# A fused LayerNorm, attention and mixture-of-experts kernel: other groups, and another engine, for the LayerNorm scale and shift of the prologue

## The reference

```python
x = hidden_states                                  # (8, 512, 128)
xn = (x - mean(x)) / sqrt(var(x) + 1e-5)           # over the last axis
s  = attention(xn)                                 # 8 heads of 16; then its own norm, Wo, bo
# the two experts of a token come from its first two normalised elements:
h   = mod(int(xn[:, 0] + xn[:, 1]), 8)
sel = (h, mod(h + 1, 8))
g  = silu(sum over e in sel of 0.5 * (relu(xn @ W1[e] + b1[e]) @ W2[e] + b2[e]))
out = x + s * g
```

## Time and profile before

| what | value |
|---|---|
| time, median of 3 runs | 422.58 us (422.43 to 423.55) |
| time of the profiled execution | 423.16 us |
| its span, first to last instruction | 421.3 us |
| TensorE busy in the span | 389.6 us (92%) |
| VectorE | 300.1 us (71%) |
| ScalarE | 268.5 us (64%) |
| GpSimd | 153.2 us (36%) |

### The profile page before, as it was taken

How to read it: one execution, slowest core, us unless ns; L and a number is a source line. 1 busy time by engine, 2 the same in 40 slices (tenths; PEclk the granted TensorE clock), 3 DMA queues, 4 the chain that set the end, 5 groups by cost and what they waited for, 6 DMA issues and landing times.

```text
span 421.3 us, 8389 instructions
## 1 busy us (share of the span) xinstructions
PE 389.6 (92%) x2575; PEld 249.2 (59%) x2576; DVE 300.1 (71%) x793; ACT 268.5 (64%) x667; POOL 153.2 (36%) x188
## 2 busy tenths in 40 slices
PE   4986979999999999999999999999999999999984
PEld 1343868655676657666665668666666657663322
DVE  6797886667687766866676768766686767766884
ACT  3571556666667765577765767576665668575783
POOL 7753302172235442374335421642353232420100
PEclk9997799999999999999999999999999999999997
DMA  7974763244305640235504540344255141214840
GB/s 243 343 226 116 196 217 90 75 112 140 133 13 167 197 143 14 77 109 160 186 16 130 173 137 18 128 137 157 61 163 172 25 161 49 78 19 127 299 165 25
DMA packets 36946, 54.76 MB, mean 130 GB/s; under 512 B 6724, under 2 KB 25141, under 8 KB 36903
## 3 DMA queue, kind: packets, MB, share of 16 engines
q1 hardware_dynamic: 31456, 46.94, 33.5%
q0 software_dynamic: 3296, 6.76, 7.6%
q10 hardware_dynamic: 2151, 0.53, 0.6%
HBM read 15.59 MB, written 6.75 MB: 53 GB/s over the span
## 4 chain that ended last, share of the span: by engine, by line
PE 76%; DVE 11%; ACT 4%; issue 4%; DMA 2%; POOL 2%; DVEq 0%; ACTq 0%; POOLq 0%
PE ring L1383 14%; PE ring L1404 14%; PE pv_bank L1317 13%; PE score L1279 13%; PE exp L1304 11%; DVE neg_max L1034 4%; PE ring L1241 2%; PE ring L1343 2%; PE ring L1266 2%; PE ring L1325 1%; ACT hT L813 1%; ACT xin L775 1%; DMA qs<-max_rows 1%; DMA xs<-xn_rows,inverse 1%; PE ring L1365 1%
## 5 line engine op out<-in xcount | busy, mean ns | idle before, releaser
L1034 DVE TENSOR_REDUCE neg_max<-score 128x1 f32<-128x512 f32 x256 | 170.7, 685 | 70.2 <-PE score L1279 65.3
L1279 PE MATMUL score<-ks,qs 96*128 96x512 bf16 x256 | 98.4, 388 | 8.6 <-DVE neg_max L1034 7.4
L775 ACT ACTIVATE xin<-exp 128x512 f32<-128x512 f32 x120 | 70.1, 604 | 39.0 <-PE exp L1304 36.2
L1304 PE MATMUL exp<-qs,ks 99*128 99x512 bf16 x244 | 91.8, 380 | 3.2 <-ACT xin L775 1.5
L813 ACT ACTIVATE hT<-ring,pair 128x128 f32<-128x128 f32 x256 | 73.5, 375 | 28.1 <-PE ring L1383 25.4
L775 ACT ACTIVATE probs<-exp 128x512 f32<-128x512 f32 x124 | 72.8, 611 | 28.3 <-PE exp L1304 26.9
L679 POOL DMA_INDIRECT y_rows<-y_sb,inverse x32 | 32.0, 999 | 137.8 <-DVE y_sb L1166 136.6
L1404 PEld LDWEIGHTS ring<-w_sb,hT 128*128 128x128 f32 x568 | 74.2, 193 | 8.7 <-issue 2.1
L1404 PE MATMUL ring<-w_sb,hT 128*128 (+1 forms) x568 | 76.4, 278 | 0.8 <-ACT hT L813 0.8
L1383 PEld LDWEIGHTS ring<-xsT,pair 128*128 128x128 f32 x512 | 65.1, 191 | 13.8 <-issue 7.9
L1383 PE MATMUL ring<-xsT,pair 128*128 128x128 f32 x512 | 69.4, 278 | 0.5 <-issue 0.5
(11 more groups left out here) (195 smaller groups left out, 409.3 us busy)
## 6 DMA issues: line engine op xcount, KB each, us to landing
pair<-table SPq DMA_DIRECT2D x32, 580.0 KB
qs<-parts SPq DMA_DIRECT2D x42, 128.0 KB
ks<-parts SPq DMA_DIRECT2D x42, 128.0 KB
xin<-_attn_hidden_states_dram SPq DMA_DIRECT2D x8, 256.0 KB, 5.5
table<-in_L_ffn_W_dram SPq DMA_DIRECT2D x2, 1024.0 KB, 9.8
w_sb<-in_L_ffn_W_dram SPq DMA_DIRECT2D x8, 256.0 KB, 6.1
xn_rows<-xn SPq DMA_DIRECT2D x8, 256.0 KB, 3.1
table<-_attn_hidden_states_dram SPq DMA_DIRECT2D x8, 256.0 KB, 4.7
```

Source lines behind the costliest of these rows:

```text
L775: a.activation(prob(n), exp_banks[n][:, :], ACT.Exp, scale=SCALE).then_inc(exp_done, 1)
L1034: v.tensor_reduce(neg_max[:, b % 2, col:col + 1], score_bank[n % 2][:, :], AX.X, ALU.max, negate=True).then_inc(max_taken, 1)
L1279: t.matmul(score_bank[n % 2][:, :], qs[0:MAX_ROW, b % STK, hh, c * P:(c + 1) * P], ks[0:MAX_ROW, b % STK, hh, :], start=True, stop=True).t ...
L1304: t.matmul(exp_banks[n][:, :], ks[0:KROWS, b % STK, hh, kc * P:(kc + 1) * P], qs[0:KROWS, b % STK, hh, :], start=True, stop=True).then_inc ...
```

## The change

The groups become five (batch 0, batch 1, batches 2 and 3, 4 and 5, 6 and 7), with a step time for each. For all groups but the last, `shift` is computed on GpSimd, in two instructions: -mean ahead of the power, and the product with rstd behind it, for which GpSimd waits on its own power. For the last group it stays on VectorE. The sum v01 is written otherwise: x0 + x1 of all tokens is taken once, on VectorE, ahead of its wait for the last power, and `count_groups` then multiplies by rstd and adds 2 * shift, where it multiplied both elements by rstd, added shift to both and summed.

```diff
-LN_GROUPS = ((0, 1), (1, 3), (3, 6), (6, 8))
+LN_GROUPS = ((0, 1), (1, 2), (2, 4), (4, 6), (6, 8))
-SHIFT_AT = (-58.5, -56.5, -51.5, -50)
+SHIFT_AT = (-58.5, -57.5, -55.5, -53.5, -50)
...
# GpSimd, step "shift"
                     pool.wait_ge(stats_ready, end)
+                    if end < B:
+                        g.tensor_scalar(shift[:, tok], mv[:, tok, 0], -1.0, None, ALU.mult)
                     link(g.tensor_scalar(var_eps[:, tok], mv[:, tok, 1], EPS, None, ALU.add))
                     g.tensor_tensor(rstd[:, tok], var_eps[:, tok], neg_half[:, 0:C * (end - first)],
                                     ALU.pow).then_inc(rstd_ready, 1)
+                    if end < B:
+                        pool.wait_ge(rstd_ready, s[1] + 1)
+                        g.tensor_tensor(shift[:, tok], shift[:, tok], rstd[:, tok], ALU.mult).then_inc(shift_ready, 1)
...
# VectorE, count_groups
                 dve.wait_ge(iota_ready, 1)
-                two = cmp[:, 0:2 * NT].rearrange("p (t k) -> p t k", k=2)
-                link(v.tensor_tensor(two, xin[:, :, 0:2], rstd[:, :].unsqueeze(2).to_broadcast([P, NT, 2]), ALU.mult))
-                link(v.tensor_tensor(two, two, shift[:, :].unsqueeze(2).to_broadcast([P, NT, 2]), ALU.add))
-                link(v.tensor_tensor(v01[:, :], two[:, :, 0], two[:, :, 1], ALU.add))
+                dve.wait_ge(pair_summed, 1)
+                link(v.tensor_tensor(v01[:, :], v01[:, :], rstd[:, :], ALU.mult))
+                dve.wait_ge(shift_ready, len(LN_GROUPS))
+                link(v.scalar_tensor_tensor(v01[:, :], shift[:, :], 2.0, v01[:, :], ALU.mult, ALU.add))
...
# VectorE, step "shift"
+                    if end < B:
+                        continue
                     tok = slice(C * first, C * end)
+                    v.tensor_tensor(v01[:, :], xin[:, :, 0], xin[:, :, 1], ALU.add).then_inc(pair_summed, 1)
                     dve.wait_ge(rstd_ready, g + 1)
```

More of the change, by code:

```diff
@@ L381, in gated_attention_moe @@
         shift_ready = sem("shift_ready")
+        pair_summed = sem("pair_summed")
         b1_loaded = sem("b1_loaded")
```

## The result

The changed kernel took **420.20 us** (median of 20 runs, 418.54 to 421.61) against 422.69 (20 runs of before beside them, 421.05 to 423.82): ratio 0.9942, 95% interval [0.9929, 0.9955]. It is faster, by 0.58% or 2.45 us, where 1.35 was forecast. The two kernels were run beside each other twice more: 0.9956 [0.9931, 0.9981] and 0.9966 [0.9947, 0.9986]. The mean of the three is 0.9955, 1.9 us. The profiled execution took 421.46 us with a span of 419.6 us; TensorE was busy for 387.6 us.

A forecast was written before the change was run, and what follows sets the result against it. The prologue was taken as bound by the VectorE and TensorE chains meeting at `invert`, TensorE bounding the work behind it. An earlier `invert` gave 422.58 - 1.35 = 421.2 us, range 420.4 to 422.7 us.

The forecast's parts named there:

- VectorE's chain: Prologue, statistics to counts: statistics end 1.25 us earlier, `v_abs` another 0.39 us, the whole chain about 1.6 us earlier.
- rival 3: Prologue: GpSimd falls behind; a product of 0.70 us leaves no gain, 1.155 us gives 424.4 us; chance 0.04.
- The meeting at `invert`: Prologue, where VectorE's and TensorE's chains meet: TensorE's is later, `invert` ends at 30.6 us instead of 31.95, gaining 1.35 us.
- rival 2: Prologue: VectorE's whole gain arrives, 1.6 us, up to 2 if the gather overtakes small loads: 420.8 us; chance 0.14.
- Rival 1: Prologue: TensorE's chain without its 1.49 us cover, or a held gather, gives only 0.6 us: 422.0 us; chance 0.28.
- The gather: Behind `invert`: starts at 31.45 us, takes 4.78 us again, lands at 36.25 us.
- rival 4: Behind the thin stretch: the clock's return from 1.2 GHz, 2.7 us later, eats 1.35 us: 422.6 us; chance 0.09.

The follow-up runs named there:

- the early rows: The changed kernel with the bias rows loaded ahead of wq and wk on ScalarE's queue: 420.05 us, ratio to before 0.9970.
- both warm ones: The changed kernel with 28 unread matmuls around the first scores and first tile, run twice: 417.17 us (0.9900 to before) and 418.86 us (0.9913).
- `a_front`: The changed kernel with six unread matmuls behind the second score and no others: 418.75 us, ratio to before 0.9945.
- `a_small_sp`: The changed kernel with ten small loads issued by SyncE behind the last xn store instead of by ScalarE: 421.47 us, ratio to before 0.9973.
- `aw_small_late`: The changed kernel with 28 unread matmuls, plus the ten small loads issued by SyncE behind the second expert's weights: 420.42 us, ratio to before 0.9950.
- `a_warm`: The changed kernel with 28 unread matmuls behind the first six scores and ahead of the first tile: 417.17 us, ratio to before 0.9900.
- `a_again`: The changed kernel, unmodified, run again beside before: 419.16 us, ratio 0.9956.
- the warm pair: Before and the changed kernel, each with the same 28 unread matmuls: 418.62 us (0.9943 to before) and 417.17 us (0.9900).

## Why the prediction was wrong in size and right in kind

**VectorE's chain: as forecast.** In the first profile the instruction behind the statistics starts at 14.98 (14.8 forecast), the product costs 0.20 us where 0.3 was taken, the last power ends at 17.14 (17.0 forecast), `v_abs` starts at 17.3 to 17.7 in the profiles (17.5), and the counts end at 20.78 in the first profile (20.65). GpSimd waits 0.28 us before the last group, so rival 3 is excluded: it would have needed a product of 0.70 us. For the product GPSIMD Engine Reference of the Trainium skill (section 4.1, Engine selection) has GpSimd at about twice VectorE's time for two inputs; here it took 0.20 us against 0.17 for VectorE's fused shift of the same tile, so for 4 or 8 columns the factor did not show.

**The meeting at `invert`: right on the mean, not in each execution.** Forecast 30.6. The nine profiles of the changed kernel's prologue (after, its two repeats, the early rows, both warm ones, `a_front`, `a_small_sp`, `aw_small_late`) have 31.61, 30.46, 30.28, 30.09, 30.18, 30.65, 30.67, 30.67 and 30.50: mean 30.57, against 31.85 to 31.93 in five of before. That the mean meets the forecast so closely has luck in it. TensorE was free for `invert` at 29.74 in before (30.05 less the wait of 0.31), not at 29.6; and where it waits for nothing, `invert` starts at 29.0 to 29.2 and takes 1.47 us (30.14 in the first profile), where 28.8 and 1.8 were taken.

The nine are two cases. In four (30.09 to 30.50) VectorE's chain is still the late one, as rival 2 has it, and up to 1.8 us are gained; in five TensorE's is, as the forecast has it. They go with the time at which the clock first rises: at 14.9 to 15.5 us in the four, at 16.7 to 17.1 in the next four, at 17.6 in the first profile. In the five of before it rises anywhere from 14.3 to 17.9, and `invert` ends within 0.1 us of the same time: that is the cover. Rival 1's mechanism, the lost cover, is real and cost about 1.2 us in the first profile against the mean of the other eight; there the rows of `ffn_b` were last and the two-product stretch at 16.29 still took 1.70 us instead of 1.02. TensorE: Matmul & The Clock Gate of the Trainium skill (Part 1, What's actually happening) says that the point at which the clock rises varies from run to run, and the traces agree: the first products at the faster rate start at about 15.0 us in `a_warm` and at 17.8 in the first profile of after. But it did not pull the median below the forecast.

**The gather: part of it given back in some executions.** Issued 1.35 us earlier it was to last 4.78 us again. It lasted between 4.7 and 5.9 us with the loads where they are; in `a_again` 0.6 of 1.4 us were lost there. In the warm pair 1.49 of 1.67 us arrived at the first tile, but there, and in the first profile of after, the chain that ended last goes through VectorE's maxima instead, which the prediction had only moving along with `invert`.

**The step that failed** is the clock, which the sum has at nothing because of a sentence in rival 4: "The thin stretch stays as long as it was and moves as a whole, so I expect the same fall and the same return." They are not the same even in one kernel. The stretch at 1.2 GHz behind the thin one was 10.24, 6.83, 6.83 and 10.24 us in the profiles of before, its repeat and its two variants with moved loads, and 6.83, 6.83, 10.24, 10.24 and 13.65 in those of after, its two repeats and its two variants. So a term of 3.4 us up or down at 0.35 us a us, 1.2 us, nearly as large as the forecast, stood in the sum as 0; and the rival had the clock only as a loss.

Whether the change itself moves that term is not shown. In the profiles it has no less of that stretch than before. Over the timed runs before spent 10.50, 9.92, 10.07, 9.71 and 9.49 us at half clock, 9.99 over 120 runs, and after 8.87, 8.84 and 9.19, 8.95 over 44. That is 1.0 us less with an interval of 0.1 to 2.0, and an unknown part of it lies at the end of the kernel. At 0.27 to 0.35 us each, 1.0 us would be a gain of some 0.3 us. With the 1.45 us between the warm kernels this gives 1.75 us, estimated; the three comparisons mean 1.9. The 1.45 with its interval of 0.7 to 2.6 could also hold all of the 1.9, or the 1.35.

**What stays open.** The first comparison's 2.45 us is 0.5 above that mean. Its interval and that of the third barely overlap, and the rest of each profile scatters by more than that (from the 61st of VectorE's maxima to the 256th it takes 277.9 to 279.6 us, whatever the kernel). So it stays open why that comparison came out higher than the two others, in whose intervals 1.35 lies. Nor is it shown that, or why, the changed kernel spends less time at half clock: the one account I tested fell. The range ended 0.2 us above the result, since it had no term for a gain by the clock and took in rival 2 only to 420.4.

## What to carry to other kernels

A wait of one engine that hides another's lateness is cover; when a change removes it, look for what varied beneath it, because that now decides in some executions. When TensorE falls idle for a few us, price the half clock behind it as a term of its own with both signs (some 0.3 us per us here), and measure a change once with the clock held up, with enough runs: 9 and 6 gave 1.45 us for the chain, known to about 1 us only. Compare several profiles of one kernel before reading a wait in one of them, since here the late chain changed with the execution. A product of 8 columns cost 0.20 us on GpSimd against 0.17 for VectorE's shift of that size; next to the waits that it took off VectorE that was nothing.

## What the runs showed of the hardware

Matmuls that nobody reads made the kernel faster: 28 of them, of 256 columns, took the time at half clock from 10.07 to 2.69 us and before's time to 0.9943 of itself; with the change they made the best version of the study, `a_warm`, 417.17 us, 0.9900 [0.9871, 0.9929] (0.9913 when repeated). Six of them gave 0.2% (0.9945 against 0.9966 beside each other, with intervals that overlap).

The same load of the rows of `ffn_b` landed between 5.7 and 7.1 us in executions whose issue order ahead of it was the same. And a software gather of one tile lasted from at most 4.06 us, with the small loads out of its way, to 6.76 us with them issued just ahead of it and beside it from another queue.

The clock's first rise came at 14.3 to 17.9 us in profiles of kernels whose work ahead of it differed by little, and its stretch at 1.2 GHz behind the thin stretch took 3.41 us in one profile, 6.83, 10.24 or 13.65 in others. The half clock at the end of the kernel took nothing to 5.9 us; where it caught the last product, that took 2.07 us instead of 1.16.
